# Half 0's mixture added in TensorE's banks, its norm on ScalarE alone, four weight remainders ahead, half 1's products on GpSimd

## What is computed

```python
x = x + tanh(g_xattn[0]) * wkv(w, u, k=_layernorm(x), v=ctx)        # per channel, a scan over 64 tokens
x = x + tanh(g_ffn[0])   * ffn(_layernorm(x), w_gate_up, w_proj)    # ternary weights, silu(gate) * up, rms norm
x = x + tanh(g_xattn[1]) * attention(_layernorm(x), ctx, mask)
x = x + tanh(g_ffn[1])   * (fp8(_layernorm(x)) @ weight.T + bias)

def step(carry, kv_t):                      # wkv: numerator p, denominator q
    y = (A * p + E * vt) / (A * q + E)      # E = exp(u + kt - no), A = exp(o - no)
    return (A2 * p + E2 * vt, A2 * q + E2, no2), y

def ternary_quant(w, g=64):                 # bf16, one scale for each 64 weights
    scale = clip(mean(abs(w_g)), 1e-8, None)
    return clip(round(w_g / scale), -1, 1) * scale
```

## Time and profile before

| | us |
|---|---|
| median of 3 runs (lowest to highest) | 140.72 (139.71 to 140.81) |
| the profiled execution, its own time | 141.18 |
| its span | 139.4 |
| PE busy (matmuls) | 119.2, 86% |
| DVE busy | 116.5, 84% |
| ACT busy | 85.5, 61% |
| POOL busy | 32.7, 23% |

### The profile page before, as it was taken

The page is one execution under the profiler, slowest core; times in us unless marked ns, Lnnn a source line. Parts: engine busy times, 40 slices in busy tenths (PEclk is TensorE's granted clock), DMA queues, the critical chain, the costliest instruction groups (busy, mean ns, idle before and its releaser), DMA issues.

```text
span 139.4 us, 2211 instructions
## 1 busy us (share of the span) xinstructions
PE 119.2 (86%) x733; PEld 79.6 (57%) x743; DVE 116.5 (84%) x278; ACT 85.5 (61%) x163; POOL 32.7 (23%) x75
## 2 busy tenths in 40 slices
PE   5899788862899899999987999999996779496992
PEld 5799673420522346477653667777675657274581
DVE  5896999997993969999987897769997789995880
ACT  3197898028584777685765777856654534522962
POOL 7913000005000000000233802059334624401000
PEclk9999999995555999999999999999999999999999
DMA  4999950000000000000000000000000000000026
GB/s 132 288 353 350 388 131 2 0 0 0 0 0 0 0 5 2 0 0 0 0 5 0 2 0 0 5 0 0 0 2 5 0 0 0 2 0 0 2 97 208
DMA packets 7110, 6.90 MB, mean 50 GB/s; under 512 B 1336, under 2 KB 6842, under 8 KB 7098
## 3 DMA queue, kind: packets, MB, share of 16 engines
q1 hardware_dynamic: 7088, 6.75, 15.1%
q10 hardware_dynamic: 10, 0.00, 0.0%
HBM read 5.70 MB, written 1.05 MB: 48 GB/s over the span
## 4 chain that ended last, share of the span: by engine, by line
PE 47%; DVE 32%; issue 7%; ACT 6%; DMA 3%; POOL 2%; ACTq 1%; POOLq 0%; DVEq 0%
PE ps L848 8%; PE ps L849 7%; PE ps L907 5%; DVE xs L1214 4%; DVE stats L1125 4%; PE ps L1101 4%; PE ps L881 4%; DVE sums L1156 3%; PE ps L770 3%; PE ps L768 3%; DMA gate_row<-_L_ffn_weight_scale_dram 3%; DVE xn L1137 3%; PE ps L813 2%; PE ps L994 2%; DVE hbuf L1294 2%
## 5 line engine op out<-in xcount | busy, mean ns | idle before, releaser
L848 PE MATMUL ps<-wT,xhi 128*128 128x512 bf16 x60 | 23.8, 396 | 1.3 <-ACT xlo L545 1.0
L849 PE MATMUL ps<-wT,xlo 128*128 128x512 bf16 x60 | 23.5, 392 | 0.2
L907 PE MATMUL ps<-wT,wgu_raw 128*128 128x256 bf16 x128 | 16.6, 273 | 0.1
L418 POOL TENSOR_SCALAR ve<-mv 128x2 f32<-128x2 f32 (+2 forms) x12 | 2.3, 192 | 59.4 <-DVE mv L1131 59.3
L907 PEld LDWEIGHTS ps<-wT,wgu_raw 128*128 128x128 f16 x128 | 12.4, 98 | 1.6 <-DVE wgu_raw L1281 0.3
L1125 DVE BATCH_NORM_STATS2 stats<-xs 128x6 f32<-128x256 f32 x32 | 12.3, 414 | 1.1 <-DMA xs<-in_x_dram 0.7
L586 ACT ACTIVATE wgu_raw<-ps 128x512 f16<-128x512 f32 x16 | 9.6, 597 | 5.5 <-PE ps L881 5.0
L534 ACT ACTIVATE wscale<-ps 128x1024 bf16<-128x1024 f32 x6 | 6.1, 1023 | 10.3 <-PE ps L770 10.3
L1137 DVE TENSOR_SCALAR xn<-xs,mv,rstd 128x256 f32<-128x256 f32 x26 | 9.5, 409 | 2.9 <-POOL rstd L419 2.1
L1294 DVE SCALAR_TENSOR_TENSOR hbuf<-ps,pscale,sil 128x512 f32<-128x512 f32 x11 | 8.2, 749 | 3.3 <-PE ps L849 3.3
L848 PEld LDWEIGHTS ps<-wT,xhi 128*128 128x128 f16 x64 | 6.4, 100 | 7.7 <-ACT xlo L545 1.5
(11 more groups left out here) (173 smaller groups left out, 281.9 us busy)
## 6 DMA issues: line engine op xcount, KB each, us to landing
wgu_raw<-in_L_ffn_w_gate_up_dram SPq DMA_DIRECT2D x4, 512.0 KB, 9.0
ctx_sb<-in_ctx_dram SPq DMA_DIRECT2D x2, 512.0 KB, 7.3
wp_raw<-in_L_ffn_w_proj_dram SPq DMA_DIRECT2D x1, 1024.0 KB, 10.2
out_dram<-xs SPq DMA_DIRECT2D x3, 256.0 KB, 2.2
xs<-in_x_dram SPq DMA_DIRECT2D x2, 256.0 KB, 2.9
xs<-in_x_dram SPq DMA_DIRECT2D x1, 512.0 KB, 6.7
wlin_raw<-in_L_ffn_weight_dram SPq DMA_DIRECT2D x1, 256.0 KB, 9.1
out_dram<-xs SPq DMA_DIRECT2D x2, 128.0 KB, 2.0
```

Of the source, the lines that this page charges most:

```text
L848: pe.matmul(ps[:, bank, :], xhi[:, h, c, o:o + P], w, start=(c == 0), stop=False)
L849: mm = pe.matmul(ps[:, bank, :], xlo[:, h, c, o:o + P], w, start=False, stop=(c == CH - 1))
L907: mm = pe.matmul(proj_at(i), part[:, n % 2, j * P:(j + 1) * P], wT[:, GU_PAIRS + f, j * C:(j + 1) * C], start=(first and f == 0 and j == 0 ...
```

## The change

- **Mixture of half 0.** `mix_x` has TensorE multiply x by the identity into banks 0 and 1, in place of the six warm-up matmuls. `mix_y` adds `y` times `ident_tg`, the identity scaled by tanh(g), in place of `y_back(0)`. ScalarE evicts the sum to the residual (`mix_in`), and `mix_out` on VectorE is gone; `mix_stats` reads the statistics a bank at a time.
- **Norm of half 0.** ScalarE applies it to all four tiles; VectorE's two are gone.
- **Remainders.** Those with n = 1 and n = 3 use banks 4 and 5, the others banks 6 and 7 (`REST_BANK`). Four are made before unit 0; `weight_rest(4)` moves from unit 1 to unit 0. `rest_in(2)` moves ahead of the splits, `invert(2)` behind them. The maximum of the scales goes to bank 1.
- **Half 1's products** (`wkv_product(2)`, `(3)`) go from VectorE in unit 3 to GpSimd, ahead of the power for half 0's norm, released by `den_scan(2)`.
- **Smaller things.** The memset of `group_spread` goes from GpSimd to VectorE; ScalarE makes `ident_tg` before the decay columns; waits follow.

In the diff the declarations of the new tile and the three semaphores are left out.

```diff
@@ -62,6 +62,7 @@
     QUANT_ORDER = [0, 1, 4, 2, 3, 5]
+    REST_BANK = [6, 4, 6, 4, 6, 6]
     SCALE_ROWS = 24
@@ -393,7 +398,6 @@
-            pool.memset(group_spread[:, :, :], 0.0).then_inc(spread_0, 1)
             pool.wait_ge(spread_0, 1)
@@ -419,8 +423,18 @@
+            def wkv_product(k):
+
+                v = ctxT[:, k % CH, CT:NTOK].rearrange("p (b t) -> p b t", t=T)
+                pool.wait_ge(ctxT_ready, k + 1)
+                pool.wait_ge(G_ready, k + 1)
+                pool.tensor_tensor(kv[:, k, 1, :, 1:T + 1], kv[:, k, 0, :, 1:T + 1], v, ALU.mult).then_inc(GV_ready, 1)
+
             power(0, 0, TPC, 1)
             power(0, TPC, TPC, 2)
+            pool.wait_ge(den_scanned, 1)
+            wkv_product(2)
+            wkv_product(3)
             power_and_shift(1, 0, TPC, 1)
@@ -488,6 +502,9 @@
             act.preload_act_table_set("natural_log_exp_and_others")
+            act.wait_ge(ident_ready, 1)
+            act.wait_ge(tg_ready, 1)
+            act.activation(ident_tg[:, :], ident[:, :], ACT.Copy, scale=tg[:, 0:1]).then_inc(ident_tg_ready, 1)
             act.wait_ge(cols_ready, 2)
@@ -530,9 +547,14 @@
                 p = QUANT_ORDER[n]
+                bank = REST_BANK[n]
                 act.wait_ge(rest_ps, n + 1)
-                act.activation(wscale[:, p, :].rearrange("p (a b) -> p a b", a=2), ps[:, 6:8, :],
+                act.activation(wscale[:, p, :].rearrange("p (a b) -> p a b", a=2), ps[:, bank:bank + 2, :],
                                ACT.Copy).then_inc(rest_ready, 1)
+
+            def mix_in(b):
+                act.wait_ge(mix_ps, b + 1)
+                act.activation(res[:, 2 * b:2 * b + 2, :].rearrange("p i c -> p (i c)"), ps[:, b, :], ACT.Copy).then_inc(mix_ready, 1)
@@ -556,14 +578,19 @@
             invert(1)
+            mix_in(0)
+            mix_in(1)
             rest_in(0)
             rest_in(1)
-            invert(2)
-            ln_apply(1, 0, TPC // 2, 1)
+            act.wait_ge(mix_ready, 2)
+            ln_apply(1, 0, 2, 1)
+            ln_apply(1, 2, 2, 1)
+            rest_in(2)
             xn_high(0)
...
             xn_low(1)
+            invert(2)
             invert(3)
@@ -629,7 +656,6 @@
                 if n == 0:
-                    rest_in(2)
                     rest_in(3)
@@ -759,12 +785,12 @@
                     pe.wait_ge(neg_ready, 2)
-                else:
-                    pe.wait_ge(rest_ready, n)
+                if n >= 2:
+                    pe.wait_ge(rest_ready, (0, 0, 1, 2, 3, 5)[n])
                 pe.wait_ge(wsc_ready, 1)
...
                 for a in range(2):
-                    bank = 6 + a
+                    bank = REST_BANK[n] + a
                     pe.matmul(ps[:, bank, :], group_spread[:, SCALE_ROW[p] // 2 + a, :], scales[:, :],
@@ -773,7 +799,7 @@
                 pe.wait_ge(scale_max_ready, 1)
-                t = pe.transpose(ps[:, 4, 0:16], scale_max[:, :].broadcast_to([16, P]), ident[0:16, 0:16])
+                t = pe.transpose(ps[:, 1, 0:16], scale_max[:, :].broadcast_to([16, P]), ident[0:16, 0:16])
                 t.then_inc(gspread_ps, 1)
@@ -786,11 +812,8 @@
-                if h == 0:
-                    pe.wait_ge(ctxT_ready, CHUNKS * CH)
-                else:
-                    pe.wait_ge(rest_ready, PAIRS)
-                    pe.wait_ge(wl_f, 1)
+                pe.wait_ge(rest_ready, PAIRS)
+                pe.wait_ge(wl_f, 1)
                 for i in range(TPC):
@@ -798,15 +821,36 @@
+            def mix_x():
+                pe.wait_ge(in_x[0], 16)
+                pe.wait_ge(in_x[1], 16)
+                pe.wait_ge(G_ready, CHUNKS * CH)
+                for i in range(TPC):
+                    o = (i % 2) * C
+                    pe.matmul(ps[:, i // 2, o:o + C], ident[:, :], xs[:, i, :], start=(i % 2 == 0), stop=False,
+                              skip_group_check=True)
+
+            def mix_y():
+                pe.wait_ge(y_ready, CH)
+                pe.wait_ge(ident_tg_ready, 1)
+                for i in range(TPC):
+                    for c in range(CH):
+                        o = (i % 2) * C + c * P
+                        mm = pe.matmul(ps[:, i // 2, o:o + P], y[:, c, i * P:(i + 1) * P], ident_tg[:, :], start=False,
+                                       stop=(i % 2 == 1 and c == CH - 1), skip_group_check=True)
+                    if i % 2:
+                        mm.then_inc(mix_ps, 1)
+
             def ffn_in(k):
...
                 bank = XN_BANKS[k // 2][k % 2]
-                pe.wait_ge(res_ready[1], (1, 1, 2, 3)[k])
-                if k == 0:
-                    pe.wait_ge(xn_ready_act, 1)
+                if k < 2:
+                    pe.wait_ge(ctxT_ready, CHUNKS * CH)
+                    pe.wait_ge(xn_ready_act, k + 1)
                 else:
-                    pe.wait_ge(xn_ready[1], k)
+                    pe.wait_ge(res_ready[1], k - 1)
+                    pe.wait_ge(xn_ready[1], k - 1)
                 for c in range(CH):
@@ -830,7 +874,7 @@
                 elif q < 2:
-                    pe.wait_ge(xn_ready_act, q + 2)
+                    pe.wait_ge(xn_ready_act, q + 3)
                 else:
@@ -851,9 +895,12 @@
                 if n == 0:
-                    pe.wait_ge(G_ready, CHUNKS * CH)
+                    pe.wait_ge(mix_ready, 2)
+                    pe.wait_ge(mv_ready[1], 1)
+                    pe.wait_ge(xlo_ready, 1)
+                    pe.wait_ge(wq_ready, WQ_GATE[0])
+                if n == 2:
                     pe.wait_ge(xlo_ready, 2)
-                    pe.wait_ge(wq_ready, WQ_GATE[0])
                 if n == TPC:
@@ -867,6 +914,7 @@
                     pe.wait_ge(wq_ready, WQ_UP[0])
+                    pe.wait_ge(gmax_done, 1)
                 if n == TPC:
@@ -890,7 +938,7 @@
                 if n == 0:
-                    pe.wait_ge(gmax_done, 1)
+                    pe.wait_ge(rest_ready, 4)
                     pe.wait_ge(wT_ready, PAIRS)
@@ -1007,18 +1055,17 @@
             pe.wait_ge(G_ready, CHUNKS * CH)
-            keep_warm(WARM_FRONT, 0, wabs)
+            mix_x()
             for p in range(PAIRS):
                 weight_sums(p)
-            y_back(0)
-            weight_rest(0)
-            weight_rest(1)
+            mix_y()
+            for n in range(4):
+                weight_rest(n)
             spread_scales()
...
             ffn_in_left(1)
-            weight_rest(2)
             for n in range(UNITS + 2):
@@ -1051,8 +1098,6 @@
                 if n == 0:
-                    weight_rest(3)
-                if n == 1:
                     weight_rest(4)
@@ -1217,14 +1262,22 @@
-            def mix_out():
-                dve.wait_ge(tg_ready, 1)
-                dve.wait_ge(yT_ready, 2)
-                residual(1, 0, TPC, lambda i: ps[:, XN_BANKS[0][i // 2], (i % 2) * C:(i % 2 + 1) * C], lambda i: tg[:, 0:1], 1)
+            def mix_stats():
+                last = None
+                for i in range(TPC):
+                    if i % 2 == 0:
+                        dve.wait_ge(mix_ready, i // 2 + 1)
+                    now = step(dve.bn_stats(stats[:, i, :], res[:, i, :]))
+                    if i > 0:
+                        after(last)
+                        step(dve.bn_aggr(mv[:, 1, i - 1, :], stats[:, i - 1, :]))
+                    last = now
+                after(last)
+                dve.bn_aggr(mv[:, 1, TPC - 1, :], stats[:, TPC - 1, :]).then_inc(mv_ready[1], 1)
             def mix_pair(k):
-                dve.wait_ge(yT_ready, k + 1)
-                residual(1, 2 * k, 2, lambda i: ps[:, XN_BANKS[1][k - 2], i * C:(i + 1) * C], lambda i: tg[:, 0:1], k)
+                dve.wait_ge(yT_ready, k - 1)
+                residual(1, 2 * k, 2, lambda i: ps[:, XN_BANKS[1][k - 2], i * C:(i + 1) * C], lambda i: tg[:, 0:1], k - 1)
@@ -1345,7 +1398,7 @@
                 if q < 2:
-                    dve.wait_ge(xn_ready_act, q + 2)
+                    dve.wait_ge(xn_ready_act, q + 3)
                 else:
@@ -1353,6 +1406,7 @@
             dve.memset(sign_bits[:, :], 0x80008000)
+            dve.memset(group_spread[:, :, :], 0.0).then_inc(spread_0, 1)
             dve.memset(ngparts[:, :], 0.0).then_inc(guard_rows, 1)
@@ -1367,7 +1421,7 @@
                 dve.wait_ge(gspread_ps, 1)
-                dve.tensor_reduce(gmax_all[:, :], ps[:, 4, 0:16].rearrange("p (g n) -> p g n", g=2), AX_X,
+                dve.tensor_reduce(gmax_all[:, :], ps[:, 1, 0:16].rearrange("p (g n) -> p g n", g=2), AX_X,
                                   ALU.max).then_inc(gmax_done, 1)
@@ -1414,11 +1468,9 @@
             weights_scale()
-            mix_out()
-            ln_stats(1, 0, TPC)
+            mix_stats()
             den_bonus(2)
             greatest_scales()
-            ln_apply(1, TPC // 2, TPC // 2, 1)
             den_scan(3)
@@ -1438,8 +1490,6 @@
                 if n == 3:
-                    wkv_product(2)
-                    wkv_product(3)
                     num_scan(2)
```

(4 more changed lines are left out.)

## The result

| | before | after |
|---|---|---|
| median of 20 runs, us (lowest to highest) | 140.64 (139.34 to 141.38) | 139.43 (138.45 to 141.33) |
| ratio to before, 95% interval | | 0.9924 (0.9895 to 0.9954) |
| profiled execution, us (span) | 141.18 (139.4) | 139.26 (137.4) |
| mean granted clock over the span | 0.951 | 0.975 |
| DVE, ACT, POOL busy, us | 116.5, 85.5, 32.7 | 113.0, 87.6, 37.0 |

A forecast was written before the change was run, and what follows sets the result against it. A chain across engines, not one full engine, was taken to bound 31.4 to 44.8 us, then VectorE nearly without a gap. hbuf(5) at 59.3 instead of 63.56 gains 4.25: 141.18 to 136.95, forecast 136.9, range 136.2 to 137.8.

The forecast's parts named there:

- The front: Before half 0's mixture: memset on VectorE costs nothing, mix_x's 1.7 us hides under the abs wait, sums end at 26.1.
- mix_y, evictions, statistics: Half 0's mixture: mix_y 1.76 us from 26.1, two evictions at 0.6, statistics ending at 29.8 rather than 31.0.
- The products: Half 1's two products on GpSimd: about 1.25 us each from 27.05, over at 29.6, just ahead of the power.
- Rival B: GpSimd's products overrun and delay the power: 138.1 at 2.0 us each, 139.1 at 2.5 each; chance 0.11.
- The power: Half 0's norm on GpSimd: power, shift and what waits for them keep their 2.27 us, 29.9 to 32.2.
- the prediction's last list: Profile signs: if wrong, hbuf(0) waiting for TensorE, clock 0.50 past 45, stretched GpSimd operations, or 4 us lost behind unit 5.
- ScalarE: ScalarE's tiles, splits, inverses and table before unit 0: silu(0) done at 42.15, so hbuf(0) starts there against 44.18.
- Units 0 to 5: From hbuf(0) to hbuf(5): VectorE and TensorE nearly meet, hbuf(5) starts at 59.3 against 63.56.
- The sum: Whole kernel: 4.25 us gained at hbuf(5), from the profiled 141.18 to 136.95; forecast 136.9, chance 0.45.
- rival E: Before unit 0: ScalarE's new, longer chain holds unit 0 at 44.2; gain 2.2, time 138.9; chance 0.09.
- Rival A: Clock low until 45 or later: remainder 4 and unit 1 wholly at half clock; gain 2.9, time 138.2; chance 0.14.
- a clock back by 43.4: TensorE at units 0 and 1: full clock returns at about 43.4, 6.5 us after dense work begins at 36.9.

The follow-up runs named there:

- experiment 1: Kernel after, with VectorE holding its two-input operations until GpSimd's shift is out: 140.04 us, ratio 0.993 to the kernel before.
- experiment 2: Kernel before, with only ScalarE applying half 0's norm to all four tiles, VectorE to none: 142.85 us, ratio 1.0155 to the kernel before.
- experiment 3: Kernel after, with half 1's two products back on VectorE in unit 3: 140.08 us, ratio 0.9958 to the kernel before.
- experiment 5: Kernel after, without the hold, with thirteen unused matmuls in TensorE's pauses: 140.22 us, ratio 0.9892 to the kernel before.
- experiment 9: Kernel of experiment 5 with seven more unused matmuls ahead of gate(1): 138.88 us, ratio 0.9885 to the kernel before.
- experiment 4: Kernel of experiment 1 with eight unused matmuls in TensorE's pauses: 137.93 us, ratio 0.9726 to the kernel before.
- experiment 8: Kernel of experiment 4 with half 1's two products back on VectorE in unit 3: 138.88 us, ratio 0.9799 to the kernel before.
- experiment 7: Kernel of experiment 4 with nine more unused matmuls, seventeen in all: 136.80 us, ratio 0.9724 to the kernel before.
- experiment 10: Kernel of experiment 7 with half 1's two products back on VectorE in unit 3: 137.44 us, ratio 0.9798 to the kernel before.

## Why the prediction was wrong, point by point

- **The front.** Right within 0.3 us, but by luck. The memset took 0.70 us on VectorE and is not seen in any later step, as costed. mix_x was said to lie under the wait for the abs values; in the profile after, TensorE goes from the last weight transposes through mix_x and all twelve sums without a wait, and mix_y starts at 26.43, not 26.1. The cover was not there. Half 0's y was ready at 25.44, and before, the transposes of y started 0.28 us behind it, so mix_y came some 0.7 us later than y allowed (an estimate from these two distances). That the forecast was nearly met all the same is due to the first scan, 0.77 us earlier in this execution than in the one that the forecast was made from.
- **mix_y, evictions, statistics.** Right in size: 2.05 us against 1.76, within the bounds of 1.09 and 3.4, and 3.75 us from its start to the end of the statistics against 3.7 forecast (4.79 before). But their end, 30.18 against 29.8, owes as much to luck as the front does: from the first scan to the end of the statistics both profiles take 17.93 us, so the 1.2 us that were forecast here were not gained. Over all profiles it is 17.9 to 18.2 us in the old plan and 17.4 to 17.9 in the new one.
- **The products.** Right: 2.32 us against 2.5, over before the power. Rival B fell.
- **The power: the step that failed.** "The power, its shift and what waits for them took 31.04 to 33.31 = 2.27, hence 29.9 to 32.2." They took 4.33, and 2.06 us is all that hbuf(0) is late (44.25 against 42.15). The duration was taken from a row in which VectorE was waiting for this very result, and the change removes that wait. The prediction had the rule and the row that bears it out: the first operation on GpSimd had been held for 0.4 us by den_bonus, and the Trainium skill, page "SBUF — State Buffer", section "SBUF: two separate sides", says that the pair of ports which VectorE and GpSimd share is an exclusive lock when a VectorE operation has two SBUF inputs and a GpSimd operation reads SBUF, and that whichever starts first has it for the whole instruction. The trace agrees that the two shut each other out: the power ended with den_bonus(3), and experiments 1 and 2 switch the 2.40 us off and on. It does not show the order that the page gives: the power's row starts at 30.96, ahead of the scan at 31.33, and yet it ended only behind two VectorE operations, neither of them longer than alone. I weighed that rule for the products only, which were new, and not for the power, which was old, though the change rewrote what runs beside it. The sign itself stood in the prediction's last list, "GpSimd operations stretched next to VectorE's".
- **ScalarE.** Right: from the shift to silu(0) the prediction had 9.3 us (32.2 to 41.5), the profile has 9.0 (34.60 to 43.62).
- **Units 0 to 5.** Right: 17.15 us forecast from hbuf(0) to hbuf(5), 17.10 measured, nearly all of it VectorE's own work as argued. The clock came back at about 43.0 against 43.4, but that is luck: the forecast carried over 6.5 us from the start of dense work, at 36.9, while gate(0) started at 39.75 and the clock came back 3.2 us later. What lies behind hbuf(5) took 76.05 us of the span against 75.84 before, so only 0.2 us was given back there.
- **The sum.** With the power at 4.33 us the forecast's own working gives 63.56 - 61.4 = 2.2 us less, 139.0. That is rival E in place and price (unit 0 held by ScalarE's chain, 138.9), with another cause than the one it named: ScalarE's chain was not too long, it started too late. The profiled execution came to 139.26.
- **From profile to median.** The two profiled executions are 1.92 us apart, the medians 1.2. The one before was 0.54 above the median of 20 (the prediction knew of 0.46, against its three runs), and the sum was made from it. A likely place for these 0.7 us is the front: 0.77 us of the 1.92 lie ahead of the first scan, where profiles of one plan differ by up to 1.4 us, and the 1.15 that are left are near the medians' 1.2. No run tests this.
- **The clock.** Rival A had the right mechanism and the wrong condition. It did not come true in the kernel after, where the clock was back before unit 1; it came true, and dearer, once the power was quick (experiment 1), though there the hold had a part in it. The forecast of 136.9 supposed that a quick power and a clock back by 43.4 go together. In the only kernel without filling that had the quick power they did not.
- **What the gain is made of.** With the pauses filled the change brings nothing (138.86 and 138.88): by the profiles 2.1 us are won in the units, by the removed wait before hbuf(2) and the products, and 2.7 lost before them. That the 1.1 us that were measured come from the shorter stretch at half clock, 6.9 us instead of 13.4, fits this but is argued, not shown. The forecast's claim that the old plan was bound by a chain across engines left out that filling the old plan's pauses alone was worth 1.8 us.

## What to carry to other kernels

A duration read on GpSimd holds only for what VectorE did beside it; when a change removes a VectorE wait or moves work there, look up which of its operations with two SBUF inputs now lie beside GpSimd's, and whether GpSimd's result is on the critical path. A short wait on an engine with slack can be worth more than keeping it busy. Here a wait of 1.4 us on VectorE, with the pauses filled, went with a time 2.1 us shorter. When a plan is made faster ahead of TensorE, read where TensorE's new pauses are, and fill them before judging the plan: a pair of plans compared with the clock falling in one and not in the other says little about either.

## What the runs showed of the hardware

- A power of 128x4 elements took 1.01 us on GpSimd when VectorE was idle or reduced one input (the kernel before and seven experiments), and 2.40 us beside a scan and a scalar_tensor_tensor, the same in all five kernels that had this order (the kernel after, experiments 2, 3, 5 and 9). In the front of the kernel after the same shape took 2.02 us beside two scans, and 1.02 in the kernel before. VectorE's operations in that stretch were not longer for it (scan 1.22 against 1.23): in these traces the loss was GpSimd's alone. Two operations on 128x4, 0.20 us alone and beside VectorE's one-input scaling (the kernel before, 32.82 to 33.31), took 0.52 to 0.56 beside its 16-bit tensor_tensor operations.
- GpSimd's product of two 128x512 fp32 tensors took 1.16 us, VectorE's 0.64.
- Matmuls of 512 columns that nothing uses, in TensorE's pauses, kept the granted clock at 1.00 from 17 to 64 us in seven of the eight profiles that had them, where without them it was 0.50 for 7 to 17 us. Eight were not enough: the mean clock was 1.00 in three of the six runs of experiment 4 and one of the eight of experiment 8. Seventeen gave 1.00 in all four runs of experiment 7 and five of the six of experiment 10. Nine more of them in experiment 7 left hbuf(0) and hbuf(5) where experiment 4 has them, within 0.05 us, and its four runs lie within 0.4 us.
- fp32 matmuls of 128 columns that are not transposes cost 0.26 us each (the eight of mix_y, sixteen instructions in the trace, in 2.05), transposes 0.14 (eight in 1.09).
